# Two graph layers on one core: index tables kept in SBUF, part of the mean and of the edge features computed on ScalarE

## The reference, cut to what matters

```python
h = relu(layernorm(x))
x = x + L0(h, node_vec1, edge_attr_4, edge_attr_8, ..., src, dst, 16)
h = relu(layernorm(x))
x = x + L1(h, edge_attr_4, ..., src, dst)

# L0: f = linear(h) * attr; weight = silu(edge_scalars @ fc_w1 / sqrt(8)) @ fc_w2 / 8
m0a = gs * ys * w1_                                  # gs, gv = f[src]; ys, yv = edge_attr_4
m0b = sum(gv * yv[:, None, :], -1) * INV3 * w4_
m1a = gs[..., None] * yv[:, None, :] * w2_[..., None]
m1b = gv * ys[..., None] * w3_[..., None]
mid = segment_sum(edge_feat, dst) / sqrt(16)
# result: cos(angle) * self(h) + sin(angle) * linear(mid), angle from mid
# L1: a message for each edge from h[src] and edge_attr_4, segment_sum over dst, linear, relu
```

## Time and profile before

| what | value |
|---|---|
| median of 3 runs | 2452.86 us |
| the profiled execution | 2459.89 us, span 2458.1 us |
| PE busy | 1824.8 us, 74% |
| DVE busy | 1873.4 us, 76% |
| ACT busy | 1296.0 us, 53% |
| POOL busy | 1477.5 us, 60% |
| setup, to the first product of stage 1 | 0 to 123 us |
| stage 1 | 123 to 1371 us |
| stage 2 | 1371 to 1905 us |
| stage 3 | 1905 to 2458 us |

### The profile page before, as it was taken

One profiled execution on the slowest core, in us unless ns is written; L12 is line 12 of the kernel. 1 busy time (PEld: TensorE's weight loads), 2 busy tenths in 40 slices (PEclk: granted clock), 3 DMA queues, 4 the chain that ended last, 5 costly groups with the idle time before them and its releaser, 6 DMA issues.

```text
span 2458.1 us, 51427 instructions
## 1 busy us (share of the span) xinstructions
PE 1824.8 (74%) x12730; PEld 1696.7 (69%) x12730; DVE 1873.4 (76%) x5982; ACT 1296.0 (53%) x3409; POOL 1477.5 (60%) x1432
## 2 busy tenths in 40 slices
PE   0788888888888888888888554544543788898887
PEld 0287778777787777877777544444443788888887
DVE  2099999999999999999999676666666566665564
ACT  0256666666666666666666555555555333333332
POOL 1045455554545555455553677777777777777776
PEclk9999999999999999999999755555555899998999
DMA  9445555555555555555555534334433334444443
GB/s 85 145 139 186 196 206 202 196 188 195 200 201 203 190 195 191 201 205 194 195 184 185 172 108 118 114 116 123 117 117 117 94 105 111 115 111 110 113 115 85
DMA packets 236558, 377.35 MB, mean 154 GB/s; under 512 B 116353, under 2 KB 146108, under 8 KB 236364
## 3 DMA queue, kind: packets, MB, share of 16 engines
q1 hardware_dynamic: 189484, 302.66, 39.1%
q0 software_dynamic: 47040, 74.31, 11.2%
HBM read 183.27 MB, written 201.21 MB: 156 GB/s over the span
## 4 chain that ended last, share of the span: by engine, by line
PE 33%; issue 17%; DVE 14%; ACT 12%; DMA 12%; POOL 6%; SPq 4%; ACTq 1%; DVEq 1%; POOLq 0%
ACT h L774 6%; PE bank L981 5%; DMA q_row<-row_tab 4%; PE bank L976 4%; DMA x_all<-in_xa,i_dst 3%; DVE st L1207 3%; POOL h_all L612 3%; PE bank L1090 3%; PE bank L982 3%; PE bank L1066 2%; DMA out<-yo,i_put 2%; POOL x_all L606 2%; PE bank L1158 2%; ACT h L889 2%; ACT tot L832 2%
## 5 line engine op out<-in xcount | busy, mean ns | idle before, releaser
L649 POOL TENSOR_TENSOR yo<-x,h 128x640 f32<-128x640 f32 x196 | 303.9, 1551 | 506.2 <-ACT h L774 504.9
L981 PE MATMUL bank<-wp,hT 128*128 128x160 f32 x1568 | 376.3, 322 | 0.0
L774 ACT ACTIVATE h<-x,nmr,inv 128x160 f32<-128x160 f32 x784 | 342.2, 514 | 1.5 <-DVE nmr L1211 1.5
L606 POOL DMA_INDIRECT x_e<-in_xa,i_src x192 | 210.8, 1098 | 161.1 <-issue 78.3
L981 PE MATMUL bank<-wp,eT 128*128 128x160 f32 x784 | 263.0, 428 | 51.2 <-ACT eR L897 43.7
L982 PE MATMUL bank<-wp,hR 128*128 128x64 f32 x1568 | 259.4, 247 | 0.0
L1358 DVE SCALAR_TENSOR_TENSOR x<-bank,scl,x_all 128x160 f32<-128x160 f32 x784 | 254.7, 365 | 5.1 <-PE bank L982 1.8
L982 PEld LDWEIGHTS bank<-wp,hR 128*128 128x128 f32 x1568 | 255.5, 190 | 0.0
L612 POOL DMA_INDIRECT out<-yo,i_put x196 | 209.7, 1070 | 74.3 <-issue 41.0
L612 POOL DMA_INDIRECT h_all<-h,i_put x196 | 217.4, 1109 | 59.8 <-issue 58.9
L976 PE MATMUL bank<-ident,h_e 128*128 128x128 f32 x392 | 83.9, 353 | 215.8 <-DVE hr_e L1527 215.4
(11 more groups left out here) (161 smaller groups left out, 5508.3 us busy)
## 6 DMA issues: line engine op xcount, KB each, us to landing
x_all<-in_xa SPq DMA_DIRECT2D x98, 644.0 KB, 5.0
h_all<-h SPq DMA_DIRECT2D x98, 640.0 KB, 3.0
out<-yo SPq DMA_DIRECT2D x98, 640.0 KB, 3.3
q_row<-row_tab SPq DMA_DIRECT2D x98, 256.0 KB
sum_tab<-tot SPq DMA_DIRECT2D x49, 322.0 KB, 4.2
y_tab<-yo SPq DMA_DIRECT2D x49, 320.0 KB
x<-y_tab SPq DMA_DIRECT2D x49, 320.0 KB
cv<-sum_tab SPq DMA_DIRECT2D x25, 322.0 KB, 3.2
```

What stands on the lines that cost most here:

```text
L606: nc.gpsimd.indirect_dma_start(into[:, t * width:(t + 1) * width], None, rows, bass.IndirectOffsetOnAxis(ap=index[:, t:t + 1], axis=0)).th ...
L649: nc.gpsimd.tensor_tensor(yo[j][:, a:b], x1[j][:, a:b], h1[j][:, a:b], ALU.add).then_inc(d_y, 1)
L774: ins = nc.scalar.activation(h1[j][:, k * D:(k + 1) * D], x1[j][:, k * D:(k + 1) * D], ACT.Relu, bias=nmr2[j][:, k:k + 1], scale=inv2[j][: ...
L981: nc.tensor.matmul(dst_ps, main[:, t * P:(t + 1) * P], wp[:, w:w + D], start=True, stop=False)
```

## The change

What it does, part by part:

- **Tables.** `src_tab`, `dst_tab`, `put_tab` and `key_tab` no longer exist. POOL copies the four columns of a quad from the SBUF tables `t_src`, `t_gat` or `t_put` into the small index tile (`index_copy`) and waits for its own copy. `row_tab` is copied from a host-made transposed input. The `same` matrix takes its key from `f_dst` in SBUF.
- **Carry.** `carry` is no longer a 128 x 512 comparison on DVE. It is zero but for its last row, and SP loads that row for each quad from `carry_tab`, which is computed once. The carry matmul takes 32 rows in place of 128. In stage 3 SP's `p3_tables` also waits for the sums of the quad before last (`m_seg`).
- **Hidden layer of the edge network.** Loads run up to four groups ahead, and the products wait no more for the scaled weights.
- **Scale.** `dense_scale` moves from DVE to the head of POOL's `step`.
- **Vector features.** POOL computes `scly` = scale times edge vector once a quad, ACT writes three more copies of 32 columns (stride 3) in `p1_source`, and the third DVE instruction of `p1_features` goes.
- **Mean.** DVE's `dense_centre` subtracts the mean for rows 0 to 3 of a block. ACT does rows 4 to 7 as mean - x, in four instructions, and its Relu copy of that half takes the scale -1.
- **SP's order.** `p1_tables` moves one block earlier and no longer loads keys. Loads of index tiles go.

```diff
@@ sync, setup @@
-            sp.wait_ge(s_tabc, 6)
-            sp.dma_start(src_tab.rearrange("q p c -> p q c"), ...).then_inc(s_tab_out, 16)
-            sp.dma_start(dst_tab.rearrange("q p c -> p q c"), ...).then_inc(s_tab_out, 16)
-            sp.dma_start(put_tab.rearrange("q p c -> p q c"), ...).then_inc(s_tab_out, 16)
-            sp.dma_start(key_tab.rearrange("q p c -> p q c"), f_key[:, :, :]).then_inc(s_tab_out, 16)
-            sp.dma_start(row_tab[0:TA, :], t_row[0][0:TA, :]).then_inc(s_tab_out, 16)
+            sp.dma_start(row_tab, dst_rows).then_inc(s_rows, 16)
...
-            net_load(0)
+            for g in range(4):
+                net_load(g)
+            sp.wait_ge(s_car, 1)
+            sp.dma_start(carry_tab[0:TA, :], c_row[0][0:TA, :]).then_inc(s_car_out, 16)
...
             for g in range(NB):
-                if g + 1 < NB:
-                    net_load(g + 1)
                 net_store(g)
+                if g + 4 < NB:
+                    net_load(g + 4)
@@ sync, stages @@
+            def p1_carry(q):
+                j = q.mod(2)
+                wait(sp, e_seg, q.times(GQ, -GQ))
+                sp.dma_start(carry[j][P - 1:P, :], carry_q[q.times(1)].unsqueeze(0)).then_inc(e_ca[j], 16)
...
             def p3_tables(q):
                 wait(sp, m_v, q.times(GQ, -GQ))
-                sp.dma_start(q_key[j][:, :], key_tab[q.times(1)]).then_inc(m_tb[j], 16)
+                wait(sp, m_seg, q.times(GQ, -GQ))
@@ gpsimd @@
+            def index_copy(into, table, q, signal):
+                nc.gpsimd.tensor_copy(into[:, :], table[:, bass.ds(q.times(GQ), GQ)]).then_inc(signal, 1)
+                pool.wait_ge(signal, q.times(1, 1))
...
             def p2_gather(q):
                 k = q.mod(4)
-                pool.wait_ge(r_ix[k], q.over(4, 16, 16))
+                wait(pool, r_g[k], q.over(4, 64))
+                index_copy(i_dst[k], t_gat, q, r_ix)
...
+            def dense_scale(u):
+                j = u.mod(4)
+                pool.wait_ge(d_scl, u.times(2, 1))
+                nc.gpsimd.tensor_tensor(scl1[j][:, :], inv1[j][:, :], x3(x_in[j], XW, GD)[:, :, D], ALU.mult).then_inc(d_scl, 1)
@@ scalar @@
+            def dense_centre(u):
+                act.wait_ge(d_ln1, u.times(1, 1))
+                wait(act, d_tr, u.times(2, -2))
+                x, st = x_in[u.mod(4)], st1[u.mod(4)]
+                for k in range(GQ, GD):
+                    ins = nc.scalar.activation(hb[u.mod(2)][:, k * P:(k + 1) * P], x[:, k * XW + 32:k * XW + D], ACT.Identity,
+                                               bias=st[:, k, 1:2], scale=-1.0)
+                ins.then_inc(d_cna, 1)
...
-                nc.scalar.activation(g_e[n.mod(2)][:, :], bank[5 + n.mod(2)][:, 0:D], ACT.Copy,
-                                     scale=scl_e[j][:, t:t + 1]).then_inc(e_gg, 1)
+                nc.scalar.activation(g[:, 0:D], b[:, 0:D], ACT.Copy, scale=scl_e[j][:, t:t + 1])
+                for c in range(3):
+                    ins = nc.scalar.activation(g[:, D + c:D + DV:3], b[:, DS + c:D:3], ACT.Copy,
+                                               scale=scly[j][:, 3 * t + c:3 * t + c + 1])
+                ins.then_inc(e_gg, 1)
...
                 if u.within(U):
                     dense_root1(u)
+                    dense_centre(u)
                 slot(u, 0)
@@ vector @@
-                V.tensor_tensor(x3(hb[j], P, GD), x[:, :, 32:D], bc_last(stat(st1[u.mod(4)], GD, 1), P), ALU.subtract)
+                V.tensor_tensor(x3(hb[j], P, GD)[:, 0:GQ, :], x[:, 0:GQ, 32:D], bc_last(stat(st1[u.mod(4)], GQ, 1), P),
+                                ALU.subtract)
...
-                else:
-                    v.wait_ge(e_fm, n.times(1, 1))
-                    V.tensor_tensor(f[:, 224:320].rearrange("p (u i) -> p u i", i=3),
-                                    f[:, 224:320].rearrange("p (u i) -> p u i", i=3),
-                                    bc_mid(ed(j, t, 1, 4), DU), ALU.mult).then_inc(e_ft, 1)
```

281 lines of the change are left out of this document (128 added, 153 removed).

## The result

| | median, us | range | runs | profiled execution | its span |
|---|---|---|---|---|---|
| before | 2452.73 | 2452.57 to 2453.29 | 4 | 2459.89 | 2458.1 |
| after | 2743.95 | 2737.43 to 2750.5 | 4 | 2740.19 | 2736.9 |

The changed kernel takes 1.1187 times as long (95% interval 1.1156 to 1.1218). The forecast was 2560 us with a range to 2640: the sign was right and the size was not.

What follows compares the result with a forecast made beforehand. Stage 1 was taken as bound by the PE and ACT path, stages 2 and 3 by POOL. Setup -44, stage 1 +79 and index copies +72 made +107 us: 2567 profiled, 2560 us median, range 2475 to 2640.

Steps and rivals of the forecast that it cites:

- Setup, -44: Setup: first hidden-layer product starts at 24 us (-40), four loads in flight close gaps between products (-4).
- The rival with full clock: Hidden layer in the setup: no more gaps, so products run at full clock, -20 us more, 2540 us; chance 12%.
- DVE leaves PE's path: Stage 1: PE's wait for DVE's features vanishes, at most -0.84 us for each two blocks, 25.4 to 24.6 us.
- the bound was 41: Stage 1: -41 us if ACT's new instructions vanish in its waits and DVE's 0.84 us for two blocks is gained.
- ACT's addition, +79 in stage 1: Stage 1: ACT's subtractions and strided copies delay `tot`; two blocks take 27.1 us against 25.4, +79 us in all.
- The carry product keeps its 161 columns at 32 rows, and I take it at the same price: Stage 1: the carry product on 32 rows costs the same as before, no change.
- Index copies at 0.40 us: Stages 2 and 3: POOL's 196 waited-for copies at 0.40 us, 78 us, less 6 for the missing comparison: +72.
- one more issue gap: Stages 2 and 3: upper bound for an index copy, a whole issue gap more, 0.58 us each, 114 us.
- SyncE's tables in stage 3, "0, up to +40": Stage 3: tables wait for the sums, mostly covered by POOL's longer quad: 0, up to +40 us if not.
- One sum over stages: Whole kernel: setup -44, stage 1 +79 and index copies +72 simply added to +107 us.
- -13 us on 2453: Rival, ACT's work hides: its short instructions fall into ACT's waits in stage 1, -13 us, 2442 us; chance 9%.
- +263: Rival, ACT costs in full: no overlap, DVE's stalls stay, -44 + 235 + 72, 2715 us; 12% in full or halfway.

Runs made afterwards that it cites:

- e4: The changed kernel with the hidden layer's products on 128 rows, POOL clearing two tiles first: 2725.51 us.
- e17: e8 with half of the dense rows' mean taken off on ACT, `scl1` staying on DVE: 2393.8 us.
- e8: The changed kernel with index copies a quad ahead, stage 3's carry load waiting separately, 128-row products, ACT's added work back on DVE: 2407.65 us.
- e11: e8 with ACT making the three strided copies of g_e, as in the changed kernel: 2434.81 us.
- e3: The changed kernel with the carry products of stages 1 and 3 on all 128 rows again: 2655.76 us.
- e9: e8 with the 32-row carry products of the changed kernel in stages 1 and 3: 2429.77 us.
- e2: The changed kernel with POOL's index copies of stages 2 and 3 made a quad ahead, not waited for at once: 2642.52 us.
- e13: e8 with SyncE waiting for the sums ahead of all three loads of a stage 3 quad: 2485.38 us.
- e14: The changed kernel with four unused 128x512 products added per stage 3 quad, ahead of the transposes PE waits for: 2695.2 us.
- e15: e8 with the small product `scl1` moved to POOL, without ACT's subtractions: 2550.66 us.

## Why the prediction was wrong, step by step

- **Setup, -44: right** (-47). The start at 24 us and the half speed of the hidden layer came as forecast. The rival with full clock needed not only no gaps, as I had it, but 128 rows: e4 gave 14 us more, not 20.
- **DVE leaves PE's path: right.** PE's wait for features is gone (0.1 us in 900). Relieving DVE of half the subtractions gains 12 us, with ACT's work for it already paid (e17 against e8); the bound was 41 for all of DVE's relief.
- **ACT's addition, +79 in stage 1: right in mechanism, too large.** Measured +56 and a slot of 6.67 us for 6.78. The prices of the instructions were right: the subtractions were forecast at 0.395 us and the copies at 0.29, and they take 0.392 and 0.303. What they do to the slot was 23 us too large, and which step of the slot was mis-sized stays open. With 128-row products the subtractions alone cost -12 us (e17) and the copies alone +26 (e11), both together +55 (e3 against e8), so the two don't have a price each, as I gave them.
- **"The carry product keeps its 161 columns at 32 rows, and I take it at the same price": wrong.** It takes 347 ns, and the 128-row form 299. Beside ACT's work this cost nothing (e3), without it 28 us of stage 1 (e9), and with late tables 83 us of stage 3. The Trainium skill, TensorE: Matmul & The Clock Gate, section "Why this matters for your kernels", says that a single product with 32 rows takes as long as one with 128. The runs differ: 347 against 299 ns in stage 1, at the same granted clock.
- **Index copies at 0.40 us: the first large miss.** The range was 0.28 to 0.58, from small operations that wait for one another. What follows here is an indirect DMA, and it starts 0.89 us after the copy's end: 1.10 us from DMA to DMA in place of 0.30, a price of 0.80. So my upper end, "one more issue gap", was no bound. The trace before had a nearer row than the one I took, right behind it in the same timeline of POOL in stage 1:

```profile
718.89 0.20 POOL L669 TENSOR_TENSOR scl_e<-inv_e,x_e 128x4 f32<-128x4 f32 x1
720.04 1.07 POOL L606 DMA_INDIRECT x_e<-in_xa,i_src  x1 [0.96 <-issue]
```

An indirect DMA behind a small operation of POOL starts 0.96 us after its end. With this gap a copy would have cost 0.19 + 0.96 - 0.30 = 0.85 us, 167 us for 196, and the forecast would have been about 2650. (That DMA doesn't wait for the operation ahead of it, and what fills its 0.96 us isn't shown.) Stage 2: +88 us for 98 copies, of which e2 gives back 79.
- **SyncE's tables in stage 3, "0, up to +40": the second.** I took the existing wait of 73 us for `q_row` as a sign that there was slack. It was no slack of the loads: three loads behind a later event took 75 us alone (e13). Cover was named (POOL's longer quad) and never worked out as a loop: sum, then load, then comparison, then the next sum.
- **One sum over stages: wrong in form, the third miss.** Stage 3 was forecast as +36 and measured +181, and its causes don't add: own waits 70, late tables 75, both 98, and with the 32 rows 181. The term for the clock was missing altogether. PE wasn't the bound of stage 3, so I priced its stalls at nothing; the clock that fell with them is worth some 45 us (e14). The Trainium skill, same page, section "HAM oscillation — how this bites in real kernels", describes the kind: a wait for a DMA in each tile lets the clock fall, and the next tile starts slow. The trace agrees at 2120 us, where PE has waited 1.72 us: 0.95, then 0.56. Here PE waits for DVE's features, and only DVE for the DMA.
- **Two sums of the rivals** are off by a microsecond or two: -13 us on 2453 is 2440 and not 2442, and +263 is 2716 and not 2715. Nothing hangs on it.

## What to carry to other kernels

An instruction's price is that of what stands behind it: a 0.2 us copy costs 0.06 us when it is made a quad ahead and 0.80 to 0.90 us when the next indirect DMA waits for it. Look in the trace for the row of that very pair, the small operation and the DMA behind it, before taking the row of another pair. Before a load is put behind a later event, write out the loop that it closes, and don't read an existing wait on that load as slack. Where a change touches several loops of one stage, their costs can overlap or reinforce each other (75 and 70 us made 98, and 32 rows that cost nothing alone made it 181); build the version with all of them undone and put the parts back one by one.

## What the runs showed of the hardware that I hadn't expected

- A product with 32 rows is slower than one with 128 of the same columns: 347 against 299 ns at a granted clock of 1.00 (128 x 161).
- In the setup it is 0.81 against 0.53 us (512 columns), but there the level differs too. The clock's column shows 1.00 through those 42 us of 32-row products; the transposes right behind them take 1.12 us for four, which is their time at the 1.2 GHz level (stage 2 has 1.11, where the column shows 0.53; stage 1 has 0.63 to 0.66), so the column doesn't show the level there. The level alone can account for this difference (1.12 / 0.63 is more than 0.81 / 0.49).
- Added work can shorten a kernel: 384 products more, 49 us less, with the granted clock of stage 3 at 0.99 in place of 0.81.
- DVE's 128x1024 subtraction takes 2.41 us in place of 1.22 where it begins while a POOL addition of 1.53 us runs, 48 times of 98 in e15.
- A 0.20 us operation moved from DVE to POOL cost between 0 and 139 us, according to what DVE still had to do in the same block. The reason of the larger part stays open.
